# Differential attention, layer 0: both halves of a tile turned in one group of eight, the first head's matrix made beside the layer norm, the split of the FFN weight moved behind

## What is computed

```python
XN = layernorm(X)                                   # 2 x 1024 x 128
for h in range(8):                                  # Wq, Wk, Wv: 256 rows per head
    Q1, Q2 = XN @ Wq[h].T                           # each 128 wide; K1, K2 likewise
    lam = exp(sum(lq1 * lk1)) - exp(sum(lq2 * lk2)) + 0.8 - 0.6 * exp(-0.3)
    attn = softmax(Q1 @ K1.T * s) - lam * softmax(Q2 @ K2.T * s)    # s = 1 / sqrt(128)
    O = attn @ (XN @ Wv[h].T)                       # 256 wide
    O = O / sqrt(mean(O * O) + 1e-5) * rms_scale * (0.2 + 0.6 * exp(-0.3))
    out += O @ Wo[:, h].T
X = X + out * silu(ffn(XN))                            # w1, w2, h1, h2, w3
```

## Time and profile before

| | us |
|---|---|
| median of 3 runs (lowest, highest) | 1997.31 (1994.69, 2002.84) |
| the profiled execution | 2003.42 |
| its span, first to last instruction | 2001.4 |

### The profile page before, as it was taken

One profiled execution on the slowest core, in us unless ns is written; L12 is line 12 of the kernel. 1 busy time (PEld: TensorE's weight loads), 2 busy tenths in 40 slices (PEclk: granted clock), 3 DMA queues, 4 the chain that ended last, 5 costly groups with the idle time before them and its releaser, 6 DMA issues. The chain is left out here.

```text
span 2001.4 us, 34480 instructions
## 1 busy us (share of the span) xinstructions
PE 1751.3 (88%) x13199; PEld 1432.8 (72%) x13199; DVE 1445.7 (72%) x2911; ACT 1154.3 (58%) x2342; POOL 1038.7 (52%) x995
## 2 busy tenths in 40 slices
PE   5999999999999999699789789875598657999997
PEld 3888888888888888577656577764477634666675
DVE  6888888888888888243567677758667488777772
ACT  3677666767676666355457655543243344666665
POOL 3889898989898998640122223434347530111111
PEclk9999999999999999899889899976799869999999
DMA  2000000000000000100000000002035400000000
GB/s 83 14 1 14 1 14 1 14 1 14 1 1 1 1 1 1 28 26 0 20 7 20 6 1 2 2 2 89 22 80 137 95 15 0 2 2 1 2 2 23
DMA packets 50372, 37.44 MB, mean 19 GB/s; under 512 B 7496, under 2 KB 43624, under 8 KB 50208
## 3 DMA queue, kind: packets, MB, share of 16 engines
q1 hardware_dynamic: 43520, 30.53, 5.2%
q0 software_dynamic: 5632, 4.20, 1.5%
q10 hardware_dynamic: 1056, 0.52, 0.1%
HBM read 29.99 MB, written 5.24 MB: 18 GB/s over the span
## 5 line engine op out<-in xcount | busy, mean ns | idle before, releaser
L673 POOL TENSOR_TENSOR dtl<-dts,dth 128x512 fp32r<-128x512 f32 x256 | 339.1, 1325 | 20.5
L605 DVE TENSOR_REDUCE nm<-PS 128x1 f32<-128x1024 f32 x256 | 311.4, 1216 | 18.7 <-PE PS L203 17.3
L1770 ACT ACTIVATE ET_a<-PS 128x256 f32<-128x256 f32 (+2 forms) x512 | 221.7, 496 | 123.9 <-PE PS L1669 75.5
L671 POOL CAST dth<-dts 128x512 fp32r<-128x512 f32 x256 | 247.3, 966 | 68.4 <-ACT dts L538 68.4
L201 PE MATMUL PS<-xh,yh 128*128 128x512 f32 x512 | 224.0, 438 | 7.1 <-ACT G L531 4.6
L144 PE MATMUL PS<-C,XN 128*128 128x128 f32 x1120 | 177.3, 284 | 42.0 <-DVE XN L196 40.4
L203 PE MATMUL PS<-xh,yl 128*128 128x512 f32 x512 | 202.4, 395 | 0.0
L202 PE MATMUL PS<-xl,yh 128*128 128x512 f32 x512 | 201.5, 394 | 0.0
L1589 POOL TENSOR_SCALAR_AFFINE_SELECT ET_a<-ET_a 128x1024 f32<-128x1024 f32 x32 | 35.0, 1094 | 305.1 <-ACT ET_a L1770 305.1
L531 ACT ACTIVATE XNT<-PS,nm 128x1024 f32<-128x1024 f32 x128 | 143.6, 1122 | 83.7 <-DVE nm L605 83.6
L531 ACT ACTIVATE G<-PS,nm 128x1024 f32<-128x1024 f32 x128 | 142.9, 1116 | 76.7 <-DVE nm L605 76.2
(11 more groups left out here) (415 smaller groups left out, 4736.0 us busy)
## 6 DMA issues: line engine op xcount, KB each, us to landing
e_wg<-in_WgT SPq DMA_DIRECT2D x16, 256.0 KB
e_wu<-in_WuT SPq DMA_DIRECT2D x16, 256.0 KB
e_wd<-in_WdT SPq DMA_DIRECT2D x16, 256.0 KB
wqn<-in_L_attn_Wq SPq DMA_DIRECT2D x8, 128.0 KB, 2.1
wkn<-in_L_attn_Wk SPq DMA_DIRECT2D x8, 128.0 KB, 2.4
wvn<-in_L_attn_Wv SPq DMA_DIRECT2D x8, 128.0 KB, 2.5
won<-in_WoT SPq DMA_DIRECT2D x8, 128.0 KB, 2.5
wvt<-in_WvT SPq DMA_DIRECT2D x8, 128.0 KB, 2.7
```

The source lines that it names most:

```text
L605: e.tensor_reduce(self.nm[:, half, i:i + 1], self.S[half], AX.X, MAX, negate=True).then_inc(*self.top.up((g, half)))
L671: e.tensor_copy(hi, src).then_inc(*ts.up((g, g4, "h")))
L673: e.tensor_tensor(lo, src, f(hi), SUB).then_inc(*ts.up((g, g4, "l")))
L1770: e.activation(dst, src, ACT.Exp, scale=self.SC, bias=0.0).then_inc(*self.ex.up(it))
```

## The change

- TensorE's step becomes scores(g, 1), weigh(g - 8), scores(g, 0), job, meet, turn(g - 2, 0), turn(g - 2, 1): all eight transposes in one go. The z product comes one step later (g - 5 for g - 4), the u/o product and all behind it too (TAIL 8). ScalarE's two copies in step g are of tile g - 3, both halves; GpSimd splits both halves of tile g - 3. `gather` falls on odd steps.
- GpSimd's `factors` is cut in two: the two operations on the sums of the exponentials in step 3 of eight, the other three in step 0; `add` moves to the steps 1 and 2, `weights` to step 8 of sixteen. The exponentials of unit u wait for the first half of unit u - 2's factors.
- Head 0's M is made in `Start`: two products of two matmuls ahead of the transposes, into ZB; mh on ScalarE between the square root and the lambda exponential, ml on VectorE behind the fourth normalised tile; the first quarter of xl behind the twelfth. The square root's table load and the root come before the lambda exponential. What is left of `prep(0)` becomes the job of step 2.
- w1 is loaded into ST instead of XNT; GpSimd splits it behind the split of XN and head 0's weights, which change places; `add` waits for it, the exponentials no longer do.

Cut to its core:

```diff
     def sp(self, e, q):
-        e.dma_start(k.XNT[:, 0:512], k.A["w1T"]).then_inc(*self.in_w1.up("w"))
+        e.dma_start(self.w1, k.A["w1T"]).then_inc(*self.in_w1.up("w"))
...
     def pe(self, e, q):
                  stop=True).then_inc(*self.lam_sum.up("s"))
+        self.attn.head0_pe(e, q)
         for c in range(4):
...
     def act(self, e, q):
         q.wait_ge(self.in_c, "c")
+        k.preload(e, 0)
+        k.root(e, q, self.ln, self.sq, 0)
+        self.attn.head0_act(e, q)
         q.wait_ge(self.lam_sum, "s")
         e.activation(lm[:, 0:2, :], k.bank(7)[:, 0:16].rearrange("p (i h) -> p i h", i=2), ACT.Exp, scale=1.0,
                      bias=0.0).then_inc(*self.lam_exp.up("e"))
-        k.preload(e, 0)
-        k.root(e, q, self.ln, self.sq, 0)
...
     def dve(self, e, q):
+        for i in range(NT):
+            k.scaled(e, k.X, k.XN, i).then_inc(*self.ln.up(("n", i)))
+            if i == 3:
+                self.attn.head0_dve(e, q)
+            elif i == 11:
+                low(0)
+        for c in range(1, 4):
+            low(c)
...
+    def head0_pe(self, e, q):
+        q.wait_ge(self.in_w[0], (0, 4))
+        for half in range(2):
+            t = e.matmul(self.ZB[:, 128 * half:128 * half + 128], self.wqn[:, 0, half, :], self.wkn[:, 0, half, :], start=True, stop=True)
+        t.then_inc(*self.head0.up("m"))
+
+    def head0_act(self, e, q):
+        q.wait_ge(self.head0, "m")
+        e.activation(self.mh[:, 0, :, :], self.ZB.rearrange("p (c d) -> p c d", c=2), ACT.Copy).then_inc(*self.p_high.up((0, "m")))
+
+    def head0_dve(self, e, q):
+        q.wait_ge(self.p_high, (0, "m"))
+        e.tensor_tensor(self.ml[:, 0, :, :], self.ZB.rearrange("p (c d) -> p c d", c=2), f(self.mh[:, 0, :, :]),
+                        SUB).then_inc(*self.p_low.up((0, "m")))
...
     def pe(self, e, q):
         for g in range(self.NG + self.TAIL):
             if live:
                 scores(g, 1)
-            if 0 <= g - 7 < self.NG:
-                weigh(g - 7)
-            if mid:
-                turn(g - 2, 0)
+            if 0 <= g - 8 < self.NG:
+                weigh(g - 8)
             if live:
                 scores(g, 0)
             if g in self.jobs:
                 run(self.jobs[g])
-            if 0 <= g - 4 < self.NG:
-                meet((g - 4) // 2, g % 2)
-            if mid:
+            if 0 <= g - 5 < self.NG:
+                meet(*divmod(g - 5, 2))
+            if 0 <= g - 2 < self.NG:
+                turn(g - 2, 0)
                 turn(g - 2, 1)
...
     def act(self, e, q):
-            else:
-                q.wait_ge(s.w1_split, "l")
+            if u >= 2:
+                q.wait_ge(self.factor, (u - 2, 0))
...
             if 0 <= g - 3 < self.NG:
+                turn(g - 3, 0)
+            if 0 <= g - 8 < self.NG:
+                square(g - 8)
+            if g % 2 and 0 <= (g - 7) // 2 < self.NG // 2:
+                gather((g - 7) // 2)
+            if 0 <= g - 3 < self.NG:
                 turn(g - 3, 1)
...
     def pool(self, e, q):
-        weights(0)
         e.tensor_copy(self.xnh[:, :, :], k.XN[:, :, :]).then_inc(*self.x_split.up("h"))
         q.wait_ge(self.x_split, "h")
         e.tensor_tensor(self.xnl[:, :, :], k.XN[:, :, :], f(self.xnh[:, :, :]), SUB).then_inc(*self.x_split.up("l"))
+        weights(0)
+        s.split_w1(e, q)
         for g in range(self.NG + self.TAIL + 4):
-            if g >= 15 and g % 8 == 7:
-                factors((g - 15) // 8)
+            if g >= 16 and g % 8 == 0 and g < 8 * self.U + 16:
+                factors((g - 16) // 8, False)
+            if g >= 11 and g % 8 == 3 and g < 8 * self.U + 11:
+                factors((g - 11) // 8, True)
             if 0 <= g - 3 < self.NG:
+                split(g - 3, 0)
                 split(g - 3, 1)
-            if 0 <= g - 2 < self.NG:
-                split(g - 2, 0)
-            if g % 16 == 7 and g // 16 + 1 < self.H:
+            if g % 16 == 8 and g // 16 + 1 < self.H:
                 weights(g // 16 + 1)
-            if g >= 16 and g % 8 in (0, 1) and g < 8 * self.U + 16:
-                add((g - 16) // 8, g % 8)
+            if g % 8 in (1, 2) and 17 <= g < 8 * self.U + 19:
+                add((g - 17) // 8, g % 8 - 1)
```

More of the change, by code:

```diff
@@ L282, in dve, with low @@
         q.wait_ge(self.ln, (0, "r"))
-        for i in range(NT):
-            k.scaled(e, k.X, k.XN, i).then_inc(*self.ln.up(("n", i)))
-        for c in range(4):
+        def low(c):
             cs = slice(512 * c, 512 * c + 512)
@@ L310 @@
     LI = 0.8 - 0.6 * math.exp(-0.3)
-    TAIL = 7
+    TAIL = 8
     def __init__(self, k, where, s):
@@ L346, in __init__ @@
                 self.jobs[g + 2] = ("prep", u // 2 + 1)
-        first = [("prep", 0), ("y", 0, 1, 0), ("y", 0, 0, 0)]
+        s.attn = self
+        first = [("y", 0, 1, 0), ("y", 0, 0, 0)]
+        self.jobs[2] = ("prep", 0)
         use = list(first)
         for g in range(NG + self.TAIL):
-            use += [("uo", g - 7)] if 0 <= g - 7 < NG else []
+            use += [("uo", g - 8)] if 0 <= g - 8 < NG else []
             use += [self.jobs[g]] if g in self.jobs else []
@@ L367, in __init__ @@
         self.copied = k.sig("dt_copied", grid(tiles, range(2)))
-        self.t_split = k.sig("dt_split", [(g, n, x) for g, n in [(0, 0)] + [y for g in range(1, NG) for y in ((g - 1, 1), (g, 0))] + [(NG - 1, 1)]
-                                          for x in "hl"])
+        self.t_split = k.sig("dt_split", grid(tiles, range(2), "hl"))
         self.met = k.sig("tokens_met", grid(range(NG // 2), range(2)))
@@ L415, in prep @@
             q.wait_ge(self.in_w[i], (h, 4))
-            for half in range(2):
+            for half in range(2 if h else 0):
                 e.matmul(o[:, 128 * half:128 * half + 128], self.wqn[:, i, half, :], self.wkn[:, i, half, :], start=True, stop=True)
@@ L556, in act @@
             if 0 <= g - 3 < self.NG:
-                turn(g - 3, 1)
-            if 0 <= g - 7 < self.NG:
-                square(g - 7)
-            if g % 2 == 0 and 0 <= g // 2 - 3 < self.NG // 2:
-                gather(g // 2 - 3)
-            if 0 <= g - 2 < self.NG:
-                turn(g - 2, 0)
+                turn(g - 3, 0)
[4 more added lines that the diff above has]
+            if 0 <= g - 3 < self.NG:
+                turn(g - 3, 1)
             if g < self.NG:
@@ L626, in dve @@
                 top(g, 1)
-            if 0 <= g - 7 < self.NG:
-                take_out(g - 7)
-            if g % 2 == 0 and 0 <= g // 2 - 3 < self.NG // 2:
-                gather(g // 2 - 3)
+            if 0 <= g - 8 < self.NG:
+                take_out(g - 8)
+            if g % 2 and 0 <= (g - 7) // 2 < self.NG // 2:
+                gather((g - 7) // 2)
             if 0 <= g - 1 < self.NG:
@@ L673, in split, with factors @@
             e.tensor_tensor(lo, src, f(hi), SUB).then_inc(*ts.up((g, g4, "l")))
[L675 removed]
+        def factors(u, early):
             s1, a_, b_ = self.ss[:, u % 2, 0, :], self.fa[:, u % 2, :], self.fb[:, u % 2, :]
             fs = self.factor
+            if early:
+                q.wait_ge(self.exped, (8 * u + 7, 0))
+                e.tensor_tensor(a_, s1, s1, MUL).then_inc(*fs.up((u, 0)))
+                q.wait_ge(fs, (u, 0))
+                e.tensor_scalar(a_, a_, 1e-5, None, MUL).then_inc(*fs.up((u, 1)))
+                return
             q.wait_ge(self.squared, 8 * u + 7)
[L680 to L683 removed]
+            q.wait_ge(fs, (u, 1))
             e.tensor_scalar(b_, self.sqs[:, u % 2, :], 1.0 / 256, None, MUL).then_inc(*fs.up((u, 2)))
```

24 lines of the change are left out of this document (12 added, 12 removed).

## The result

| | before | after |
|---|---|---|
| median, us (lowest, highest) | 1997.49 (1994.69, 2003.39), 5 runs | 2018.79 (2009.55, 2022.43), 5 runs |
| profiled execution | 2003.42 | 2018.4 |
| its span | 2001.4 | 2016.5 |

The ratio is 1.0093, with a 95% interval of 1.0061 to 1.0125. The forecast of 1995.2 us and no change was wrong: the time is 12 us above the range, and the sign is that of the second rival.

A forecast was written before the change was run, and what follows sets the result against it. TensorE was taken to bound the kernel, working in 98% of the attention loop. Terms -0.6 + 4.8 - 5.7 - 0.6 = -2.1 us, from 1997.31, gave 1995.2 us; range 1980 to 2007.

The forecast's parts named there:

- the second rival: Attention loop: VectorE late where TensorE has least room, step 3; both sums hit in each block, 19 us more, 2014; chance 0.13.
- I take the stalls of now: Attention loop: TensorE's stalls behind GpSimd's long sums stay 2.7 us per sixteen tiles, so no change.
- Eight transposes in one group: TensorE's loop step: merging two groups of four saves 0.005 us in each of 128 tiles, -0.6 us.
- What moves by it: Odd tiles without a y product: the z product starts earlier and waits 0.16 us for zl in 30 tiles, +4.8 us.
- One more step of depth: Loop pipeline, TAIL 8: splits, z and u/o products one step further apart; slack worth nothing, 0, between -2 and +2 us.
- GpSimd's extras: GpSimd's factors, sums and weights one step later: work and stalls unchanged, crowded stretch 0.6 us shorter.
- The bound of 5.4: Attention loop: upper bound on stalls per sixteen tiles, in us, if both sums hit VectorE in every block of eight.
- The opening: Before the loop: first scores at about 23.0 us where they are at 28.77, -5.7 us.
- the lambda and rms operations: Opening, on VectorE between xl and yl: priced at 0.5 us, done at 22.2 us.
- The clock: Opening: upper level expected kept; rival: it falls, 18 products start 0.20 us further apart, 3.6 us less gain, 1999; chance 0.07.
- The loop's end: Last chain of the attention: two small factor operations leave the crowded stretch, 0.6 us shorter, -0.6 us.

The follow-up runs named there:

- group_only: The kernel before with the transposes in one group, copies and splits of both halves of g - 3, depth, gather, factors and sums as before: ratio 1.0266.
- sums_0_1: The changed kernel with GpSimd's two long sums back in steps 0 and 1 of eight: ratio 1.0038 to the kernel before.
- group8_best: The changed kernel with the rms scaling behind ml and the sums back in steps 0 and 1, each in four operations: ratio 1.0030 to the kernel before.
- rms_early: The changed kernel with VectorE's rms scaling moved into the start, behind ml: ratio 1.0075 to the kernel before.

## Why the prediction was wrong

The prediction's own sum first, by the measured terms, at the end of the last sum. The wait for zl in the odd tiles: +7.2 us for +4.8. The stalls that it took as unchanged: +11.6 for 0, the rest of the +18.8 by which the loop from the first to the last tile's scores grew (795.3 for 776.5). The first scores: -1.7 for -5.7. The end, from tile 127's scores on: +1.9 for -0.6. Together +19.0, where -2.1 was forecast (with -0.6 for the transposes, which the runs don't show apart). So the step that failed is "I take the stalls of now, 2.7 us per sixteen tiles, as unchanged", and with it the opening's price.

The runs split the same +19.0 in another way: group_only is 55.3 us later than the kernel before (897.60 - 842.35). The changed kernel with the sums at their old steps (sums_0_1), which adds the depth, the cut factors and the opening to the group, is 47.8 us earlier than that (849.84). The move of the sums adds 11.5 (861.33). The first two are large and nearly cancel, to +7.5. The prediction had both near nothing: two errors of some 50 us, and that they cancel is luck. Together +19.0, of which what follows the attention gave 3.9 back in the profiled execution, without cause in the change.

- **Eight transposes in one group, -0.6.** Right about TensorE: a quiet tile still takes 5.63 us, and one with a y product 6.31 for 6.33. Wrong by 55 us about the group at the old depth (an estimated 17 of them the clock, at 0.50 for 6.8 us in each of six periods, some 5.7 of them with TensorE at work): I costed the transposes and the zl wait, and not that the first half's copy and split lose their step of lead. The prediction asked what stands behind the moved transposes on TensorE, said that ScalarE's copies keep their places in its order, and didn't follow the data on to the z product: one of the two copies was now of an older tile.
- **What moves by it, +4.8.** The mechanism and the wait were right, 0.17 us for 0.16; a term was missing, the 0.07 us by which the first product behind the pause is slower. Together 0.24 us in each of 30 tiles, +7.2 us.
- **One more step of depth, 0.** This failed together with the first. "no stall in the loop is for dtl, so the slack is worth nothing" was read off a kernel in which the first half had its lead. In the new order the slack is the change's whole defence, and is spent within it. It has a price too: it shifts gather to the odd steps, which the move of the sums shows (+11.5). It also pushes factors to step 0, next to the sums; that this costs is argued, since no run moves factors alone. With the sums beside it (sums_0_1) TensorE waited for dtl 4.4 us in 60 to 800 us, with the longer cut sums (group8_best) 12.3.
- **GpSimd's extras, "I take the stalls of now".** This is the step that failed by the most: 4.4 us per sixteen tiles for 2.7, in the tiles 32 to 111. The bound of 5.4 held, and the rival named the right place, step 3 with no room. It got a chance of 0.13 because I weighed how often the sums meet VectorE, and read that wrongly too: "the other was mostly missed", but in the other block of the kernel before the ratio took 0.62, 1.29 and 0.42 us. In the changed kernel they hold VectorE no longer than before (9.8 us per sixteen tiles for 10.1); what changed is the room that TensorE has when they do, and sums_0_1 shows it, 2.2 us per sixteen tiles for that one step. It could be read in the diff (gather on odd steps). The prediction had no term for what follows a wait: the clock at 0.50 behind three of the five long ones makes up some 5 of the 11.6 us, by the estimate above.
- **The opening, -5.7.** Worth 1.7 in first scores. The step that failed is "the lambda and rms operations (0.5, to 22.2)": the order now put the rms scaling beside GpSimd's long subtraction. The prediction had weighed the Trainium skill (SBUF — State Buffer, two separate sides) for the ratio alone, which has two SBUF inputs. The same section (under "Who interferes with whom") says that a VectorE operation in a two-port mode takes the shared pair too, and that a `tensor_scalar` can enter one when its operands meet the conditions; 4.48 us beside 4.51, and 0.16 with GpSimd idle, agree with it. Whether this one ran in such a mode, no run here shows.
- **The clock.** The y products followed the transposes at once, as expected, and were still 0.43 us apart (20.53 to 20.96), as far as the y products of the kernel before with its granted clock at 0.50. The upper level that I expected wasn't there. The rival had the sign; since VectorE held the scores, it cost nothing here. The 1.00 of the earlier trace rows was misread: that trace has no record of the clock before 18.59 us.
- **The loop's end, -0.6.** The two small operations did leave the chain, and it got the 0.6 us shorter: from the first of the last factors to the end of the last sum 6.65 us (from 854.68) for 7.26 (from 835.09). But the whole end of the loop took 38.9 us from tile 127's scores where it took 37.1. No run shows why. It isn't the wait for dtl, which is one of 3.5 us now and was one of 4.6 before, and rms_early, with the same order there, took 36.9; over all the runs this stretch lies between 35.2 and 42.7.

## What to carry over

When a producer's work is moved within a step, follow its data through every engine down to the consumer and count the steps of lead that each hand-over loses; a queue's slack that looks idle may be what the order lives on. An interference with another engine has two factors, how long it holds its victim and how much room the waiting engine has at that step, and moving a wait to other steps can change the second with the first as it was. A wait can also cost more than its length, if the clock falls behind it. Before a short operation is given a price, see what runs on GpSimd at that moment; where a long GpSimd operation can't be moved, cutting it in four helped in both orders tried at a depth that gave GpSimd time (1.0 and 1.3 us per sixteen tiles); VectorE then gets in between, and GpSimd waits for it.

## What was not expected of the hardware

- A VectorE operation on 2 columns took 4.48 us beside a GpSimd operation of 4.51, from 0.05 us behind its start to its end.
- The granted clock of the profile says nothing about the start of the program. This is the changed kernel, 20 to 24 and 27 to 33 us:

```profile
20.00:24.00 4.00, 2.86 (x8) 1.75 (x7) 3.96 (x6) 1.79 (x3) 3.92 (x2) 1.00 0.00 0
27.00:33.00 6.00, 5.48 (x17) 4.12 (x18) 3.05 (x4) 1.72 (x4) 3.74 (x6) 0.76 0.00 0
```

```profile
500.10:504.40 4.30, 4.25 (x20) 4.25 (x21) 0.02 (x1) 0.42 (x1) 3.68 (x3) 0.50 0.00 0
506.00:510.00 4.00, 4.00 (x24) 3.47 (x23) 3.25 (x4) 2.66 (x6) 2.30 (x3) 1.00 0.00 0
```

  The eight transposes took 1.56 us to the next product (502.88 to 504.44) where they take 0.79 at the upper level (491.73 to 492.52).
- Shorter waits brought the clock down too, but not each time: of the five of 1.9 us in the tiles 32 to 111 of the changed kernel, three did.
- Four GpSimd sums of 128x256 took 3.80 us, where one of 128x1024 takes 2.40: 0.72 to 0.75 each, but 1.72 for the one beside which VectorE's `combine` ran. A VectorE operation can hold GpSimd as well.
